# A four-layer graph network on one core: bf16 digits in runs of four, tanh for the gelu, and an earlier close of the sweeps

## What is computed

```python
def _hgt_layer(...):                      # layer 1, twice
    k, q, v = typed_linear(x, Wk, bk), typed_linear(x, Wq, bq), typed_linear(x, Wv, bv)
    att = (q[dst] * kt[edge_type, src]).sum(-1) * mu[edge_type] / sqrt(DH)
    alpha = segment_softmax(att, dst, n)
    agg = segment_sum(vt[edge_type, src] * alpha[..., None], dst, n)
    out = typed_linear(gelu(agg), Wa, ba)           # gelu: the tanh approximation
    return a * out + (1.0 - a) * x
x = layernorm(x + layer0(x)); x = layernorm(x + layer1(x))
x = layernorm(x + layer2(x)); x = layernorm(x + layer3(x))
```

## Time and profile before

| stretch of the profiled execution | us |
|---|---|
| whole execution, and its span | 10059.76, 10058.0 |
| load, count, first place to its first scatter | 0 to 190 |
| place, both runs | 190 to 2394 |
| layer 0 sweeps | 2394 to 4616 |
| first turn | 4616 to 4946 |
| attention sweep 1 with its end | 4946 to 6000 |
| t1 | 6000 to 6310 |
| attention sweep 2 | 6310 to 7349 |
| its end and t2 | 7349 to 7648 |
| plain sweeps, turns and the end | 7648 to 10058 |

### The profile page before, as it was taken

How to read it: one execution, slowest core, us unless ns; L and a number is a source line. 1 busy time by engine, 2 the same in 40 slices (tenths; PEclk the granted TensorE clock), 3 DMA queues, 4 the chain that set the end, 5 groups by cost and what they waited for, 6 DMA issues and landing times. The chain is left out here.

```text
span 10058.0 us, 59982 instructions
## 1 busy us (share of the span) xinstructions
PE 1997.3 (20%) x16162; PEld 1843.8 (18%) x16162; DVE 5828.1 (58%) x9520; ACT 3071.7 (31%) x3309; POOL 6847.6 (68%) x7186
## 2 busy tenths in 40 slices
PE   4555465651000000002500008000022000110002
PEld 3555465551000000002500007000022000100002
DVE  8777565553545554556588886788874322432225
ACT  6333143331223332232354543355431000110002
POOL 2777777777777777775477763677734777667773
PEclk9999955555555555556855558555555555555556
DMA  3511011111333333334466655566642333223332
GB/s 95 208 29 28 24 44 33 33 31 53 98 99 114 113 109 105 108 110 139 166 212 213 215 183 172 187 217 209 217 124 65 107 103 107 87 90 107 103 107 58
DMA packets 490844, 1161.90 MB, mean 116 GB/s; under 512 B 184121, under 2 KB 279692, under 8 KB 432396
## 3 DMA queue, kind: packets, MB, share of 16 engines
q0 software_dynamic: 255936, 474.70, 18.1%
q1 hardware_dynamic: 204620, 628.82, 16.6%
q10 hardware_dynamic: 29952, 54.54, 2.1%
HBM read 669.61 MB, written 487.92 MB: 115 GB/s over the span
## 5 line engine op out<-in xcount | busy, mean ns | idle before, releaser
L832 POOL DMA_INDIRECT slots<-REC,plc_idx x1664 | 1597.9, 960 | 554.3 <-issue 505.6
L1238 POOL DMA_INDIRECT l_swp_G<-table,KVI x1664 | 1573.3, 945 | 529.1 <-issue 506.3
L940 POOL DMA_INDIRECT l_G<-table,OTHI x1664 | 1581.6, 951 | 513.3 <-issue 506.2
L1490 POOL DMA_INDIRECT l2s_G<-table,OTHI x832 | 785.0, 944 | 428.9 <-issue 253.3
L1490 POOL DMA_INDIRECT l3s_G<-table,OTHI x832 | 786.2, 945 | 301.6 <-issue 253.3
L703 PEld LDWEIGHTS plc_pr<-plc_seen,plc_otf 128*128 128x128 f32 x3328 | 848.4, 325 | 21.3 <-issue 12.1
L703 PE MATMUL plc_pr<-plc_seen,plc_otf 128*128 128x49 f32 x3328 | 849.9, 410 | 11.1 <-DVE plc_seen L618 11.0
L1073 DVE TENSOR_TENSOR l_LB<-l_RE,l_G 128x64 f32<-128x64 f32 x104 | 29.4, 282 | 1024.7 <-DMA l_G<-table,OTHI 1024.5
L1340 DVE SCALAR_TENSOR_TENSOR l_swp_QS<-l_swp_QS,KEEP,l_swp_QX 128x128 f32<-128x128 f32 x1664 | 588.4, 354 | 36.0 <-DMA l_swp_QX<-queries 8.3
L1099 DVE TENSOR_TENSOR_SCAN l_X<-l_AW,l_X 128x2244 f32<-128x2244 f32 x104 | 502.5, 4831 | 3.6
L1399 DVE TENSOR_TENSOR_SCAN l_swp_X<-l_swp_AW,l_swp_X 128x2244 f32<-128x2244 f32 x104 | 501.4, 4821 | 0.1
(11 more groups left out here) (491 smaller groups left out, 9751.1 us busy)
## 6 DMA issues: line engine op xcount, KB each, us to landing
sums<-l_ROW SPq DMA_DIRECT2D x104, 1088.0 KB, 4.3
sums<-l_swp_ROW SPq DMA_DIRECT2D x104, 1088.0 KB
l_swp_QX<-queries SPq DMA_DIRECT2D x104, 1024.0 KB, 7.8
queries<-plc_zrow SPq DMA_DIRECT2D x33, 1664.0 KB
sums<-l3s_ROW SPq DMA_DIRECT2D x52, 1032.0 KB, 4.3
plc_low<-low_rows ACTq DMA_DIRECT2D x208, 256.0 KB, 3.4
sums<-l2s_ROW SPq DMA_DIRECT2D x52, 1024.0 KB, 4.4
table<-t_row SPq DMA_DIRECT2D x98, 512.0 KB
```

Of the source, the lines that this page charges most:

```text
L832: pool.indirect_dma_start(out=slots, out_offset=bass.IndirectOffsetOnAxis(ap=idx[:, c % IB, j:j + 1], axis=0), in_=g.REC[:, c * CH + j, :] ...
L940: pool.indirect_dma_start(out=G[:, c % GR, j, :], out_offset=None, in_=table, in_offset=bass.IndirectOffsetOnAxis(ap=g.OTHI[:, side(c), x: ...
L1238: pool.indirect_dma_start(out=G[:, c % GR, j, :], out_offset=None, in_=table, in_offset=bass.IndirectOffsetOnAxis(ap=index[:, c * CK + j:c ...
L1490: pool.indirect_dma_start(out=G[:, c % GR, j, :], out_offset=None, in_=table, in_offset=bass.IndirectOffsetOnAxis(ap=g.OTHI[:, k, c * CK + ...
```

## The change

There are five parts.

1. The digits become bf16 and lie in separate rows, DIG[p, key, digit, column]; a float32 copy of the low digits, LOW, remains for ScalarE and the transposes. One-hot tiles are laid out as [2 runs, width, 4 columns] (IN = 4), so that four columns' values lie side by side and `compare` reads all three operands with an innermost step of one 2-byte element; the counting row is repeated four times for that (iota_s in SBUF, iota_p in PSUM). TensorE reads the matrix of one column with a step of 4 elements, 8 bytes, and ScalarE writes one so. This holds in the count and in both place stages.
2. The count has eight buffers in place of three, and ScalarE builds olo in one chunk of four, 26 chunks in place of 34.
3. In layer 0 the last but one chunk is added up before the last chunk's logits.
4. In the attention sweeps the gathers of each half of a chunk count on a semaphore of their own; `carry` stands ahead of `multiply(., 0)`; the last but one chunk is closed within the second half of the queries of the last, and the last right behind its own maxima.
5. The gelu is x (1 + tanh(..)) with the factor 0.5 put into the weights once; the second half of the cubic, the 1 +, both reciprocals go.

```diff
 def compare(v, out, iota, number):
-    full = [P, out.shape[1], out.shape[2]]
-    return v.tensor_tensor(out, iota.rearrange("p (o w) -> p o w", o=1).to_broadcast(full),
-                           number.to_broadcast(full), ALU.is_equal)
+    full = [P, CH // IN, out.shape[2], IN]
+    return v.tensor_tensor(out, iota.rearrange("p (o w i) -> p o w i", o=1, i=IN).to_broadcast(full),
+                           number.rearrange("p (q o i) -> p q o i", o=1, i=IN).to_broadcast(full), ALU.is_equal)
...
+def column(digits, j):
+    return digits[:, j // IN, :, j % IN]
...
-        olo = s.sb("olo", [P, 3, CH, P], BF16)
-        ohi = s.sb("ohi", [P, 3, CH, NB], BF16)
+        olo = s.sb("olo", [P, OB, CH // IN, P, IN], BF16)
+        ohi = s.sb("ohi", [P, OB, CH // IN, NB, IN], BF16)
...
-            for c in range(2, NCH, 3):
-                if c >= 3:
-                    act.wait_ge(counted, c - 2)
+            for c in range(3, NCH, 4):
+                if c >= OB:
+                    act.wait_ge(counted, c - OB + 1)
                 for x in range(CH):
-                    o = act.activation(olo[:, 2, x, :], g.iota_b[:, :], ACT.Square, scale=-1.0,
-                                       bias=g.DIG[:, k, c * CH + x, 0:1])
+                    o = act.activation(column(olo[:, c % OB, :, :, :], x), g.iota_b[:, :], ACT.Square, scale=-1.0,
+                                       bias=g.LOW[:, k, c * CH + x:c * CH + x + 1])
...
-                    last = pe.matmul(pc[:, 0:NB], olo[:, c % 3, j, :], ohi[:, c % 3, j, :], start=False, stop=False,
-                                     skip_group_check=True)
+                    last = pe.matmul(pc[:, 0:NB], column(olo[:, c % OB, :, :, :], j), column(ohi[:, c % OB, :, :, :], j),
+                                     start=False, stop=False, skip_group_check=True)
...
-            for c in range(NC2 + 1):
-                if c < NC2:
-                    logits(c)
-                if c >= 1:
+            for c in range(NC2):
+                logits(c)
+                if 1 <= c < NC2 - 1:
                     add_up(c - 1)
+                if c >= NC2 - 2:
+                    add_up(c)
...
-                        in_offset=bass.IndirectOffsetOnAxis(ap=index[:, c * CK + j:c * CK + j + 1], axis=0)).then_inc(gathered[c % GR], 16)
+                        in_offset=bass.IndirectOffsetOnAxis(ap=index[:, c * CK + j:c * CK + j + 1], axis=0)).then_inc(gathered[j // QH][c % GR], 16)
...
             def multiply(c, u):
-                v.wait_ge(gathered[c % GR], 16 * CK * (c // GR + 1))
+                v.wait_ge(gathered[u][c % GR], 16 * QH * (c // GR + 1))
...
+            close_now = {QH + 4: weigh, QH + 5: add_up, QH + 6: carry}
...
                 elif j == 1:
                     v.wait_ge(squared, G + 1)
-                    link(v.scalar_tensor_tensor(out=sq, in0=sq, scalar=1.0 / c0, in1=x, op0=ALU.add, op1=ALU.mult))
-                    v.tensor_scalar(sq, sq, -2.0 * c * c0, 80.0, ALU.mult, ALU.min).then_inc(ready, 1)
-                elif j == 2:
+                    v.scalar_tensor_tensor(out=sq, in0=sq, scalar=1.0 / C0, in1=x, op0=ALU.add, op1=ALU.mult).then_inc(ready, 1)
+                elif j == 3:
                     v.wait_ge(rooted, G + 1)
-                    link(v.tensor_scalar(sq, sq, 1.0, None, ALU.add))
-                    link(v.reciprocal(sq[:, 0:3, :], sq[:, 0:3, :]))
-                elif j == 3:
-                    link(v.reciprocal(sq[:, 3:GT, :], sq[:, 3:GT, :]))
-                elif j == 4:
-                    v.tensor_tensor(x, x, sq, ALU.mult).then_inc(normed, 1)
+                    v.scalar_tensor_tensor(out=x, in0=sq, scalar=1.0, in1=x, op0=ALU.add, op1=ALU.mult).then_inc(normed, 1)
...
-                        act.activation(SQ[:, G % 2, :, :], SQ[:, G % 2, :, :], ACT.Exp).then_inc(rooted, 1)
+                        act.activation(SQ[:, G % 2, :, :], SQ[:, G % 2, :, :], ACT.Tanh, scale=C1 * C0).then_inc(rooted, 1)
```

More of the change, by code:

```diff
@@ L18 @@
 CH = 8
+IN = 4
 GT = 7
@@ L35 @@
 BIG = 1.0e30
+C0 = 0.044715
+C1 = 0.7978845608028654
 RW = 4
@@ L682, in tally_up @@
                 for j in range(CH):
-                    last = pe.matmul(pd[:, j * NB:(j + 1) * NB], olo[:, c % 2, j, :], ohi[:, c % HB, j, :],
-                                     start=True, stop=True)
+                    last = pe.matmul(pd[:, j * NB:(j + 1) * NB], column(olo[:, c % 2, :, :, :], j),
+                                     column(ohi[:, c % HB, :, :, :], j), start=True, stop=True)
                 last.then_inc(tally, 1)
@@ L1405, in carry @@
                 v.tensor_copy(X[:, 1 - c % 2, :, :, 0:1], X[:, c % 2, :, :, CK:CK + 1]).then_inc(carried, 1)
-            between = {0: (last_maximum, 0), 1: (maximum, 0), 2: (shift, 0), 3: (fall, 0), 4: (cut, 0),
-                       5: (weigh, -1), 6: (add_up, -1), 7: (carry, -1)}
-            for c in range(-1, NCK + 1):
+            front = {0: last_maximum, 1: maximum, 2: shift, 3: fall, 4: cut}
+            close = {5: weigh, 6: add_up, 7: carry}
+            close_now = {QH + 4: weigh, QH + 5: add_up, QH + 6: carry}
+            for c in range(-1, NCK):
                 for x in range(CK):
```

105 lines of the change are left out of this document (58 added, 47 removed).

## The result

The changed kernel takes **9956.76 us** (median of 4 runs, 9955.85 to 9960.08), the kernel before 10062.58 beside it (4 runs, 10060.24 to 10065.57). The ratio is 0.9895 with a 95% interval of 0.9878 to 0.9912: 105.8 us less. The forecast was 9955 us, 106 less.

The account below looks back on a forecast made before the run. POOL's indirect DMA issue was taken to bound the kernel, so only stretches without gathers count: 48 + 3 + 4.3 + 14 + 0 + 37 = 106 us off the 10061.6 median, 9955 us; range 9920 to 10003.

Parts of the forecast that it names:

- POOL bounds the sweeps and place: Place and sweeps: POOL's DMA issue sets the pace, so cheaper work inside them gains zero.
- The count, -48: Count: ScalarE paces at 3.45 us per four chunks, counts out at 117 against 165.30; bounds -3 and -50.
- a rival with a price of 22 us at half rate: Count: ScalarE's Squares writing 8 bytes apart are slow, count 22 us longer, 9977 to 9981 in all; chance 0.14.
- VectorE's rate: Compares on bf16 go at two elements a step: olo 0.65 to 0.7 us, ohi 0.36.
- the other case: VectorE keeps its old rate: count's VectorE work 139 us, gain 58 in place of 106, 10003; chance 0.12.
- The start of place, -3: Compares ahead of each run's first index: each pair 0.8 us shorter, 3 us in all; bounds 0 and -3.
- The tails, -4.3 and -14: Ends of layer 0 and the attention sweeps: last add_up 4.3 us sooner, last weigh 7.0 sooner per sweep, 14 for two.
- t1, 0: Turn after the first attention sweep: first group 7.2 us sooner, ScalarE's wait for puts grows equally; bounds 0 and -7.
- t2, -37: Turn after the second attention sweep, paced by VectorE: 24.7 us per group against 29.89; bounds -31 to -37.
- TensorE's upper clock: t2: clock rises to 2.4 GHz, VectorE bounds at 18.4 us a group, up to 31 us more, 9924; chance 0.12.

Follow-up runs that it names:

- digits_f32: The changed kernel with the digits' tile DIG back in float32, in the new layout; 10002.75 us.
- run2: The changed kernel with the count's one-hot tiles in runs of two columns in place of four (steps of 4 bytes); 9956.0 us.
- run8: The changed kernel with the count's one-hot tiles in runs of eight columns in place of four (steps of 16 bytes); 10009.55 us.
- buffers_only: The kernel before with eight count buffers and one chunk in four for ScalarE, digits still float32 pairs; 11534.05 us on a slower chip (kernel before there 11513.86).
- tails_again: The changed kernel, first attention sweep closed with the old lag, second closed early but waiting for both halves at each multiply; 9958.1 us.
- puts_between: The changed kernel with POOL in t1 issuing three groups' fetches ahead, then two fetches between puts of the queries; 9935.9 us.
- old_gelu_t1: The changed kernel with the gelu of before (Exp, two reciprocals) in t1 alone; 11447.09 us on a slower chip (kernel before there 11513.86).
- two_pg: The changed kernel with two PSUM banks for pg, the product that OWN is read from in t2; 9928.27 us.

## Why the prediction was right

- **POOL bounds the sweeps and place.** Right. Place holds 312 compares of each width, and the medians of digits_f32 there (1199 and 553 ns) against 666 and 352 make 229 us less work for VectorE; after its first index place gains 1.3 us. The sweeps of layer 0 even gave back 1.8 us.
- **The count, -48.** The mechanism was right: ScalarE's chain, one chunk in four, no wait on TensorE. The size was off by 4, and the term of the sum that was mis-sized is the Squares' 2.47 us: they take 2.67 when they write 8 bytes apart, the turn 3.63 in place of 3.45, and 26 turns of 0.18 are 4.7 us. The forecast had this as a rival with a price of 22 us at half rate (its 0.80 a turn makes 21); the rate fell by 8%. run2 and run8 show on either side of it that the step causes it.
- **VectorE's rate.** Right to 0.01 us for ohi (0.36) and within the 0.65 to 0.7 for olo. buffers_only and digits_f32 show the other case: 161.5 and 162.7, where 23.5 us of start and the 139 of VectorE's work that the prediction gave for this case make 162.5.
- **The start of place, -3.** 4.0. The compares there read their counting row from PSUM and still doubled. Line L122 in place:

```profile
L122 DVE TENSOR_TENSOR plc_olo<-fixed,DIG x208: 628/666/2691, 126.9 to 2258.0; 128x1024 bf16<-128x1024 bf16 x104
```

  666 ns on the median against 1199 in digits_f32. The Trainium skill ("VectorE: DVE Perf Modes", section on the perf-mode tier table) puts tensor_tensor with any PSUM operand at the single rate; the measurement decides against it for one bf16 source in PSUM.
- **The tails, -4.3 and -14.** 4.4 and 14.9. The walk through VectorE's order gave 14.8 us from the last issue to the last weigh; it was 14.3. tails_again shows what each half of the edit carries in the attention sweeps. The gain holds only where the sweep keeps POOL's pace.
- **t1, 0.** 0.7. The wait on the puts grew from 11.7 to 16.1 (19 was forecast, from the whole 7.2), the pitch around it by 7.8, and the start came 8.8 sooner. puts_between shows that the puts are the cause; old_gelu_t1 shows only that t1 is no shorter by the new gelu on the slower chip. The prediction's 47 pitches of 4.05 and one of 17 make 207 us and not 205.4, since a few are shorter; nothing hangs on it.
- **t2, -37.** 37.8, with 24.70 us per group as worked out. The rival, TensorE's upper clock, came for about 10 us only. Its price was summed wrong: 24.7 less 18.4 is 6.3 us a group, 38 for the six groups and not 31. The one group that ran partly at the upper level took 21.01 us. two_pg has the clock at 0.80 but 20.56 us a group and not 18.4, through another edit, the second bank; that its 30.1 us lie near the rival's 31 is chance.

That the sum came out within 0.2 us is luck. The terms are off in both directions: 4.0 too much in the count; 1.0, 1.0, 0.7 and 0.8 too little in place, the tails, t1 and t2; and 2.6 lost elsewhere. The two profiled spans differ by 103.2, the medians by 105.8.

## What to carry to other kernels

When one engine issues at a fixed pace through most of the time, count only the stretches where it is idle, and walk them in the order of the program: work taken from an engine inside its shadow (here 229 us in place and some 50 in t1, of 375) is worth next to nothing. A loop of several engines through a few buffers has to be widened and its slowest member sped up together; with ScalarE's share at one in four the buffers alone gave 4 us, the rate alone 17, both 44. And read what is queued ahead of the thing that is waited for: a gain that vanished in t1 stood behind 49 fetches, and there interleaving them was worth 19 us, the faster arithmetic 0.7.
